# Last FFN: the scale columns made inside VectorE's step operations, in place of three GpSimd products a batch; FFN 0: two GpSimd products in one

## The reference

```python
# FFN 0
def rms_norm(x): return (x - mean(x)) / sqrt(var(x) + 1e-8)
def activation_quant(x):
    s = 127.0 / max(abs(x), axis=-1)
    return clip(round(s * x), -128, 127) / s
xq = activation_quant(rms_norm(x))
out = ternary(silu(ternary(xq, W_g)) * ternary(xq, W_u), W_d)      # matmuls with sign(W)

# last FFN
def act_quant(x):
    scale = 128 / clip(max(abs(x), axis=-1), 1e-5)
    return clip(round(x * scale), -128, 127) / scale
def weight_quant(w):
    scale = 1 / clip(mean(abs(w)), 1e-5)
    return clip(round(w * scale), -1, 1) / scale
gate, up = act_quant(x) @ weight_quant(w_gate).T, act_quant(x) @ weight_quant(w_up).T
h = fwht(silu(gate) * up)              # normalised Walsh-Hadamard transform over 1024
out = act_quant(h) @ weight_quant(w_down).T
x = layernorm(x + out)
```

## Time and profile before

| | |
|---|---|
| median of 3 runs | 720.35 us (719.85 to 720.46) |
| the profiled execution | 719.75 us |
| its span | 717.8 us |
| busy in the span | TensorE 687.1, VectorE 604.6, GpSimd 540.1, ScalarE 410.9 us |
| FFN 0 | about 217 to 340 us |
| last FFN | first `f_e` at 527.5 us, last step of the tail at 713 us; the convolution's last product on TensorE at 582.6 us |

### The profile page before, as it was taken

How to read it: one execution, slowest core, us unless ns; L and a number is a source line. 1 busy time by engine, 2 the same in 40 slices (tenths; PEclk the granted TensorE clock), 3 DMA queues, 4 the chain that set the end, 5 groups by cost and what they waited for, 6 DMA issues and landing times. The chain is left out here.

```text
span 717.8 us, 13771 instructions
## 1 busy us (share of the span) xinstructions
PE 687.1 (96%) x4278; PEld 498.4 (69%) x4302; DVE 604.6 (84%) x1281; ACT 410.9 (57%) x660; POOL 540.1 (75%) x781
## 2 busy tenths in 40 slices
PE   6999999999999999999889999999999999999994
PEld 5888888755444677778668778874544458777883
DVE  2987879679999987755899999988999998878874
ACT  0566667711160654544689978980000358888985
POOL 1878979889877445351067978999998989999963
PEclk9999999999999999999999999999999999999998
DMA  7820000000400041000031211204000000000001
GB/s 272 350 101 3 2 2 2 2 1 2 175 0 1 0 170 56 1 1 2 5 124 52 81 58 44 85 1 136 1 0 1 0 2 1 9 16 16 24 16 45
DMA packets 12727, 33.39 MB, mean 47 GB/s; under 512 B 2672, under 2 KB 8048, under 8 KB 11376
## 3 DMA queue, kind: packets, MB, share of 16 engines
q1 hardware_dynamic: 12656, 32.52, 12.5%
HBM read 30.35 MB, written 2.16 MB: 45 GB/s over the span
## 5 line engine op out<-in xcount | busy, mean ns | idle before, releaser
L1053 PE MATMUL bank<-XT,win_late 128*128 128x256 f32 x320 | 79.3, 385 | 2.2 <-DVE ss_xc L1238 1.8
L619 DVE TENSOR_REDUCE MIX<-m_pr 128x128 f32<-128x1024 f32 x64 | 76.8, 1208 | 0.7 <-issue 0.2
L1238 DVE SCALAR_TENSOR_TENSOR ss_xc<-bank,cw_late,ss_xc 128x254 f32<-128x254 f32 x144 | 67.7, 476 | 3.9 <-ACT ss_xc L1142 0.4
L564 POOL TENSOR_TENSOR m_kv<-CTXT 128x512 f32<-128x512 f32 x64 | 65.1, 1042 | 7.5 <-PE bank L596 6.5
L564 POOL TENSOR_TENSOR m_kv<-XT,CTXT 128x512 f32<-128x512 f32 x64 | 67.1, 1076 | 2.3 <-PE bank L596 2.3
L594 PE MATMUL bank<-m_kv,toep 128*128 128x512 f32 x128 | 65.9, 596 | 0.9 <-DVE ss_ysum L1261 0.8
L1053 PEld LDWEIGHTS bank<-XT,win_late 128*128 128x128 f32 x320 | 57.2, 190 | 11.7 <-DVE ss_xc L1238 3.6
L595 PE MATMUL bank<-m_kv,toep 128*128 128x512 f32 x128 | 65.4, 592 | 0.0
L596 PE MATMUL bank<-m_kv,toep 128*128 128x512 f32 x128 | 65.4, 592 | 0.0
L750 PE MATMUL bank<-wd,f_pmt 128*128 128x256 f32 x256 | 60.4, 379 | 0.0
L1530 PE MATMUL bank<-had_last,f_ht 128*128 128x256 f32 x256 | 58.9, 379 | 0.0
(11 more groups left out here) (247 smaller groups left out, 1869.8 us busy)
## 6 DMA issues: line engine op xcount, KB each, us to landing
MIX<-cum_rows SPq DMA_DIRECT2D x15, 512.0 KB, 3.6
toep<-toep_dram SPq DMA_DIRECT2D x2, 2048.0 KB, 12.4
X<-x_dram SPq DMA_DIRECT2D x1, 2048.0 KB, 13.0
CTXT<-ctxT_dram SPq DMA_DIRECT2D x1, 2048.0 KB, 17.8
out_dram<-f_o SPq DMA_DIRECT2D x16, 128.0 KB, 1.7
XT<-xT_dram SPq DMA_DIRECT2D x1, 1280.0 KB, 8.7
win_late<-win_dram SPq DMA_DIRECT2D x1, 1280.0 KB, 5.2
wgu<-wgu_dram SPq DMA_DIRECT2D x1, 1024.0 KB, 5.3
```

The lines of the kernel that those rows point to most:

```text
L564: m = nc.gpsimd.tensor_tensor(KV[n % 3][:, c, :, :].rearrange("p (b j) i -> p b j i", b=HB), ki, vj, ALU.mult)
L619: nc.vector.tensor_reduce(head(MIX)[:, :, a, bass.ts(h, HB), :], PR[n % 2][:, :, :, :].rearrange("p c (b j) i -> p c b j i", b=HB), op=ALU ...
L1053: m = nc.tensor.matmul(bX[(NU * g + n) % 3][:, 0:GS_], win[:, h, off:off + P], XT[:, h, bass.ts(g, GS_)], start=(h == 0), stop=(h == C - 1))
L1238: m = nc.vector.scalar_tensor_tensor(acc[:, :, sh:S], bank[:, :, 0:S - sh], cw[:, r, n:n + 1], acc[:, :, sh:S], ALU.mult, ALU.add)
```

## The change

In the last FFN, `step_size` becomes one SCALAR_TENSOR_TENSOR on three columns: the peak, spread over the three, max 1e-5, times a constant row of three, `w128` = (1/128, mean of gate/128, mean of up/4096). Its three results are the step and the columns for `silu` and `multiply`. `v_step` does the same with two columns: the step and the column for `add_down`. `gate_scale`, `up_scale` and `down_scale` go, with their semaphores; who waited for those now waits for the step operation. ScalarE makes the constants once, three activations in place of one, and GpSimd fills the two that are 1/128 with two memsets at its entry to the stage. In FFN 0, `f_va` and `f_vb` become one TENSOR_SCALAR with two multiplications.

```diff
@@ mixer, scalar consts @@
-            nc.scalar.activation(T["ws32"][:, :], T["wscale"][:, 1:2], ACT.Identity, scale=1.0 / 32).then_inc(s["made"], 1)
+            for k, m, scale in ((1, 0, 1.0 / 128), (2, 1, 1.0 / 4096), (4, 2, 1.0 / 128)):
+                made = nc.scalar.activation(T["w128"][:, k:k + 1], T["wscale"][:, m:m + 1], ACT.Identity, scale=scale)
+            made.then_inc(s["made"], 1)
...
@@ ffn0, gpsimd rms @@
-            nc.gpsimd.tensor_tensor(VA[k][:, :], MV[k][:, 1:2], RS[k][:, :], ALU.mult).then_inc(s["va"], 1)
-            pool.wait_ge(s["va"], n + 1)
-            nc.gpsimd.tensor_tensor(VB[k][:, :], VA[k][:, :], RS[k][:, :], ALU.mult).then_inc(s["vb"], 1)
+            nc.gpsimd.tensor_scalar(VB[k][:, :], MV[k][:, 1:2], RS[k][:, :], RS[k][:, :], ALU.mult, ALU.mult).then_inc(s["vb"], 1)
...
@@ ffn1, scalar silu @@
-            act.wait_ge(s["gs_made"], n + 1)
+            act.wait_ge(s["inv_made"], n + 1)
...
@@ ffn1, vector step_size @@
-            upto(dve, s["us_made"], n - 3)
-            upto(dve, s["gs_made"], n - 3)
+            upto(dve, s["h1_made"], n - 3)
+            upto(dve, s["silu1_made"], n - 3)
             upto(dve, s["scaled"], n - 3)
-            nc.vector.tensor_scalar(INV[n % 4][:, :], MX[n % 2][:, :], 1e-5, 1.0 / 128, ALU.max, ALU.mult).then_inc(s["inv_made"], 1)
+            if n == 0:
+                dve.wait_ge(mixed["made"], 2)
+                dve.wait_ge(s["consts"], 1)
+            nc.vector.scalar_tensor_tensor(IN3[n % 4][:, :], MX[n % 2][:, :].broadcast_to([P, 3]), 1e-5, w128[:, 0:3], ALU.max, ALU.mult).then_inc(s["inv_made"], 1)
...
@@ ffn1, vector multiply @@
-            dve.wait_ge(s["us_made"], n + 1)
...
@@ ffn1, vector v_step @@
-            upto(dve, s["fs_made"], n - 3)
-            nc.vector.tensor_scalar(HI[n % 4][:, :], HM_[n % 4][:, :], 1e-5, 1.0 / 128, ALU.max, ALU.mult).then_inc(s["hi_made"], 1)
+            upto(dve, s["down_free"], n - 3)
+            upto(dve, s["sh_made"], n - 3)
+            nc.vector.scalar_tensor_tensor(HI2[n % 4][:, :], HM_[n % 4][:, :].broadcast_to([P, 2]), 1e-5, w128[:, 3:5], ALU.max, ALU.mult).then_inc(s["hi_made"], 1)
...
@@ gpsimd_order @@
-    n.mix(28); n.mix(29); n.mix(30); g.edge(6); g.gate_scale(2); n.mix(31); g.rstd(3); g.first(0); g.up_scale(1); g.second(0); g.edge(7)
-    g.up_scale(2); g.gate_scale(3); g.up_scale(3); g.rstd(4); g.first(1); g.second(1); g.rstd(5); g.gate_scale(4); g.up_scale(4); g.edge(8)
+    n.mix(31); g.rstd(3); g.first(0); g.second(0); g.edge(7); g.rstd(4); g.first(1); g.second(1); g.rstd(5); g.edge(8); g.first(2); g.second(2)
```

More of the change, by code:

```diff
@@ L658, in ffn0 @@
     ST3, MV3, VE3, RS3 = two("st3", [P, 6]), two("mv3", [P, 2]), two("ve3", [P, 1]), two("rs3", [P, 1])
-    VA, VB, VC, RS2 = two("va", [P, 1]), two("vb", [P, 1]), two("vc", [P, 1]), two("rs2", [P, 1])
+    VB, VC, RS2 = two("vb", [P, 1]), two("vc", [P, 1]), two("rs2", [P, 1])
     MX, MS, SC, INV = two("mx", [P, 1]), two("ms", [P, 1], n=4), two("sc", [P, 1]), two("inv", [P, 1], n=4)
@@ L815, in aggregate @@
                 return
-            upto(dve, s["va"], n - 1)
+            upto(dve, s["vb"], n - 1)
             upto(dve, s["normed"], n - 1)
@@ L962, in last_tiles @@
 def last_tiles(ch, T):
-    for n, shape in (("bo", [P, P]), ("had", [P, 2, 2 * P]), ("grp", [P, P]), ("bias", [P, 1]), ("ws32", [P, 1])):
+    for n, shape in (("bo", [P, P]), ("had", [P, 2, 2 * P]), ("grp", [P, P]), ("bias", [P, 1]), ("w128", [P, 5])):
         T[n] = ch.sb(n + "_last", shape)
@@ L1398, in two @@
         return [ch.sb(f"f1_{name}{k}", shape, dt) for k in range(n)]
-    bo, had, ws32 = (T[n] for n in ("bo", "had", "ws32"))
+    bo, had = T["bo"], T["had"]
     rnd, unrnd = ch.sb("f1_rnd", [P, 1]), ch.sb("f1_unrnd", [P, 1])
@@ L1410, in ffn1 @@
     MX, SC = two("mx", [P, 1]), two("sc", [P, 1])
-    INV, GS, US, HM_, HI, SH, FS = (two(n, [P, 1], n=4) for n in ("inv", "gs", "us", "hm", "hi", "sh", "fs"))
+    IN3, HI2 = two("in3", [P, 3], n=4), two("hi2", [P, 2], n=4)
+    HM_, SH = (two(n, [P, 1], n=4) for n in ("hm", "sh"))
+    INV, GS, US = ([v[:, k:k + 1] for v in IN3] for k in range(3))
+    HI, FS = ([v[:, k:k + 1] for v in HI2] for k in range(2))
+    w128 = T["w128"]
     b5, b0, b1, b4, b2, b3, bW, bQ = T["banks"]
@@ L1743, in add_down @@
             dve.wait_ge(s["downed"], n + 1)
-            dve.wait_ge(s["fs_made"], n + 1)
             upto(dve, s["o_made"], n - 1)
@@ L1768, in enter @@
             pool.wait_ge(before["x_kept"], B)
+            for k in (0, 3):
+                nc.gpsimd.memset(w128[:, k:k + 1], 1.0 / 128)
             nc.gpsimd.memset(rnd[:, :], ROUND)
@@ L1784, in edge @@
             nc.gpsimd.tensor_tensor(E[n % 2][:, :], X[:, n, :], ctx_row(T, n), ALU.mult).then_inc(s["skip_in"], 1)
[L1786 to L1807, removed]
         def rstd(n):
@@ L1825, in rstd3 @@
             nc.gpsimd.tensor_scalar(NR3[k][:, :], MV3[k][:, 0:1], RS3[k][:, :], -1.0, ALU.mult, ALU.mult).then_inc(s["offset3"], 1)
-        return calls(enter=enter, first=first, second=second, edge=edge, gate_scale=gate_scale, up_scale=up_scale, down_scale=down_scale, rstd=rstd,
+        return calls(enter=enter, first=first, second=second, edge=edge, rstd=rstd,
                      rstd3=rstd3)
@@ L2143, in gpsimd_order @@
     g.enter(); g.edge(0); n.mix(16); g.edge(1); n.mix(17); n.mix(18); n.mix(19); n.mix(20); n.mix(21); n.mix(22); g.edge(2); n.mix(23); g.rstd(0)
-    n.mix(24); g.rstd(1); g.edge(3); n.mix(25); g.up_scale(0); g.edge(4); g.rstd(2); n.mix(26); g.gate_scale(0); n.mix(27); g.edge(5); g.gate_scale(1)
-    n.mix(28); n.mix(29); n.mix(30); g.edge(6); g.gate_scale(2); n.mix(31); g.rstd(3); g.first(0); g.up_scale(1); g.second(0); g.edge(7)
-    g.up_scale(2); g.gate_scale(3); g.up_scale(3); g.rstd(4); g.first(1); g.second(1); g.rstd(5); g.gate_scale(4); g.up_scale(4); g.edge(8)
@@ L2147, in gpsimd_order @@
[L2147 to L2154, removed]
@@ L2155, in gpsimd_order @@
-    g.first(14); g.up_scale(15); g.down_scale(10); g.second(14); g.down_scale(11); g.rstd3(9); g.rstd3(10); g.down_scale(12); g.down_scale(13)
-    g.down_scale(14); g.rstd3(11); g.down_scale(15); g.rstd3(12); g.rstd3(13); g.rstd3(14); g.rstd3(15)
+    n.mix(24); g.rstd(1); g.edge(3); n.mix(25); g.edge(4); g.rstd(2); n.mix(26); n.mix(27); g.edge(5); n.mix(28); n.mix(29); n.mix(30); g.edge(6)
+    n.mix(31); g.rstd(3); g.first(0); g.second(0); g.edge(7); g.rstd(4); g.first(1); g.second(1); g.rstd(5); g.edge(8); g.first(2); g.second(2)
@@ new lines, in gpsimd_order @@
+    g.rstd(6); g.first(3); g.edge(9); g.rstd(7); g.second(3); g.rstd3(0); g.first(4); g.second(4); g.rstd(8); g.first(5); g.edge(10); g.second(5)
+    g.rstd(9); g.first(6); g.rstd3(1); g.second(6); g.edge(11); g.rstd(10); g.edge(12); g.first(7); g.rstd3(2); g.second(7); g.rstd(11); g.edge(13)
+    g.first(8); g.rstd3(3); g.second(8); g.rstd(12); g.rstd3(4); g.first(9); g.second(9); g.edge(14); g.rstd(13); g.first(10); g.second(10)
+    g.rstd3(5); g.rstd(14); g.edge(15); g.first(11); g.second(11); g.rstd3(6); g.rstd(15); g.first(12); g.second(12); g.rstd3(7); g.first(13)
@@ L2159 @@
+    g.second(13); g.rstd3(8); g.first(14); g.second(14); g.rstd3(9); g.rstd3(10); g.rstd3(11); g.rstd3(12); g.rstd3(13); g.rstd3(14); g.rstd3(15)
 AT = ("weights_in later_in pool_consts consts proj_in value_in out_in bv_spread bias_made bp_made "
@@ L2164 @@
       "g0_made g1_made u0_made u1_made silu0_made silu1_made p0_made p1_made p0_turned p1_turned p0_kept p1_kept "
-      "downed down_free stats31 stats3 eps_added3 rstd3 normed3 x_turned x_kept va vb vc rstd2 inv_made").split()
+      "downed down_free stats31 stats3 eps_added3 rstd3 normed3 x_turned x_kept vb vc rstd2 inv_made").split()
 SS = ("rows_made ones_set unit_made tap3_made tap tapped xc_made xs_turned xs_kept xds_made xdt_made cb_made cbm_made args_made floored exped m_made "
@@ L2169 @@
 F1 = ("consts mix_turned skip_made skip_free summed stats1 stats2 eps_added rstd offset normed peaks inv_made scaled shifted "
-      "q_made q_turned q_kept g0_made g1_made u0_made u1_made silu0_made silu1_made gs_made us_made "
+      "q_made q_turned q_kept g0_made g1_made u0_made u1_made silu0_made silu1_made "
       "h0_made h1_made s1_half s1_made s2_half s2_made h0_turned h1_turned h0_kept h1_kept v0_made v1_made v0_kept v1_kept "
-      "v_peaks hi_made sh_made fs_made rounded w_made w_turned w_kept downed down_free "
+      "v_peaks hi_made sh_made rounded w_made w_turned w_kept downed down_free "
       "stats31 stats3 eps_added3 rstd3 offset3 o_made skip_in").split()
```

## The result

The changed kernel takes 725.78 us in the median of 6 runs (724.94 to 727.53) against 720.33 us (6 runs, 718.77 to 720.46): a ratio of 1.0084, interval [1.0069, 1.0099]. It is slower, by 5.45 us where 2.05 was forecast, and lies above the range.

A forecast was written before the change was run, and what follows sets the result against it. TensorE's order was taken as the bound until about 703 us. The terms 1.2 + 1.4 - 0.6 + 0.05 = +2.05 us on 720.35 gave 722.4 us, range 718.9 to 725.0.

The forecast's parts named there:

- TensorE bounds, both feeders close behind: Last FFN: TensorE's order bounds until about 703 us, with GpSimd busy 76.6 and VectorE 65.3 of 80 us.
- FFN 0 at 0: FFN 0: merging two GpSimd products saves about 0.2 us a batch, covered by GpSimd's waiting, so 0.
- The step operation is held until GpSimd's instruction ends, +11.6 us: Last FFN: two-SBUF-tensor step operations on VectorE wait out GpSimd's running instruction, 29 x 0.4 = 11.6 us blocked.
- Term (1): 577.6 to 586.5 us: held `step_size(3)` and `step_size(4)` delay TensorE directly by 1.2 us; bounds 0 and 1.4.
- The wait itself, which I said would be over 1 us: TensorE's wait for VectorE's `m_pr` at 586.66, 0.48 us before the change, was to exceed 1 us.
- Term (2): After 592 us: 9.6 us of holding meets 14.7 us of idle VectorE; 15% passes, 1.4 us; bounds 0 and 3.8.
- Term (3): Last FFN: relief of GpSimd and lost waits close a quarter of TensorE's 2.4 us of gaps, -0.6 us.
- GpSimd's busy time, a sign: Whole kernel: GpSimd's busy time was to fall by some 10 us if the prediction was right.
- Term (4): Tail: `v_step(15)` runs with GpSimd idle, +0.05 us; bounds 0 and 0.1.
- much slower: Last FFN: VectorE holds GpSimd in turn, blocked time passes at 40%, 725.5 us; chance counted within 0.56 for slower.
- Faster: Last FFN: GpSimd's 6.7 us of relief closes nearly all of TensorE's gaps, 718.3 us; chance 0.13.
- Held, but hidden: Last FFN: waits fall into VectorE's idle time, or three columns are not held, about 720.1 us; chance 0.31.

The follow-up runs named there:

- e6_extra_ops: Kernel before with its products and waits, plus 48 unused one-column TENSOR_SCALARs on VectorE behind the step operations; 723.34 us, ratio 1.0056.
- e10_fewer_ops: Kernel before with 32 fewer VectorE instructions, GpSimd's 48 products taking the peak as longer TENSOR_SCALARs with the floor; 727.09 us, ratio 1.0108.
- e1_ffn0_only: Kernel before with only FFN 0's edit, two GpSimd products made one instruction; 719.17 us, ratio 0.9996.
- e3_form_only: Kernel before, products and waits kept, both one-column step operations reading 1/128 from a second SBUF tensor; 725.90 us, ratio 1.0086.
- e2_one_input: Changed kernel with step operations as TENSOR_SCALARs of three and two columns, constants the only tensor, peak a scalar operand; 727.47 us, ratio 1.0112.
- e5_two_forms: Kernel before with `step_size` a three-column TENSOR_SCALAR with immediates, `v_step` one column with the peak as scalar operand; 724.61 us in one run (before 718.94).
- e7_no_products: Changed kernel with the old one-column immediate step operations, and neither the added columns nor GpSimd's products; 720.62 us, ratio 1.002.
- e9_pad: Changed kernel plus 48 one-column VectorE memsets in the first stage, where VectorE waits for the first product; 724.79 us, ratio 1.0077.
- e11_skip_psum: Kernel before with the skip product written back to its PSUM bank, so `skip_add` reads one tensor from PSUM; 718.40 us, ratio 0.9989.
- e4_pointer_scalars: Changed kernel with each step operation split into one-column TENSOR_SCALARs, constants of the other columns as scalar operands; 722.80 us, ratio 1.0035.

## Why the prediction was wrong, step by step

- *TensorE bounds, both feeders close behind:* right. The windows, e6_extra_ops and e10_fewer_ops show both as near the bound.
- *FFN 0 at 0:* right (e1_ffn0_only).
- *The step operation is held until GpSimd's instruction ends, +11.6 us:* right in mechanism and nearly in size. It was +10.3, means of 459 and 487 ns, ends 0.02 us after GpSimd's; 11.8 in e3_form_only. The condition, two tensors from SBUF, was too narrow: one tensor of three columns is held as well (e2_one_input, e5_two_forms).
- *Term (1), 1.2 us before 586.66:* nearly in size, in part by luck. TensorE's transposes moved from 586.66 to 587.22. At the first transposes of the stage after was 0.33 us ahead (536.79 against 537.12), so it had lost 0.9 us. `step_size(3)` took 0.83 us and `step_size(4)` 0.67, as worked out, but `skip_add`, 1.49 us at 581.98 in before, took 0.67 there and gave 0.8 us back. In turn `step_size(0)` to `(2)`, put at 0, took 0.39, 0.63 and 0.37 us, and VectorE had lost 0.5 us by 577.79. The wait itself, which I said would be over 1 us, stayed at 0.43: the delay had come in earlier.
- *Term (2), "I let 15% through", 1.4 us:* this is the step that failed. After 592 us the step operations were held for 8.2 us (what each took over 0.15 us), near the 9.6 forecast, but from 586.66 to `v_step(15)` the changed kernel fell from 0.6 to 5.4 us behind. That is 4.9 us with the relief of term (3) already taken off, so some 60% or more went through in place of 15%. Of e3_form_only's held time 51% went through. I set 9.6 us of holding against 14.7 us of idle VectorE and took the idle time for slack. It took in less than half. Where VectorE of after is idle it waits for its partners (second fence below), and the holding falls into the busy runs between, ahead of a multiply or a rounding that TensorE needs (661.91, 594.17, 684.82). It also pushes other instructions of VectorE behind a butterfly: 2.6 us are lost that way between 594.17 and 599.27, of which 0.5 are won back by 602. Even the bound of 40% was too low.
- *Term (3), relief of GpSimd, -0.6:* by itself nothing (e7_no_products, +0.3 to 0.6 of span at like clock); beside a loaded VectorE -0.4 to -0.9, so the size was right there. It is inside the 4.9 us. GpSimd's busy time, a sign that I put at some 10 us less, fell by 7.1.
- *Term (4), the tail:* right, 0.17 us.
- *Not in the sum:* about 1 us outside the span, which is gone with 48 instructions more (e9_pad); its cause stays open.
- *The rivals:* "much slower", 725.5 us, has the price, though not the whole of the mechanism: GpSimd, with less to do, did not fall behind by its own work, it waited more for VectorE (in before 2.5 and 1.7 us for these two, beside 8.3 us for `f_hi` that went with the products). Waits of after from 560 to 724 us (us, times, longest), GpSimd's here and VectorE's below:

```profile
POOL f_veo L461 <- DVE f_mvo L1766: 14.2, 6, 8.8
...
POOL f_ve L461 <- DVE f_mv L1669: 7.2, 7, 2.0
```

```profile
DVE f_hm L1724 <- ACT f_v L1605: 6.2, 8, 1.3
...
DVE f_ydown L1752 <- ACT f_o L1627: 3.8, 4, 2.7
DVE f_ydown L1752 <- PE bank L1555: 2.9, 4, 1.3
```

"Faster" fell with e7_no_products: without the products the span is no shorter, so the 2.4 us of TensorE's gaps do not come from them. "Held, but hidden" fell with TensorE's 4.85 us of idle time.

## What to carry to other kernels

Where two feeders run near full beside the bound, read idle time as the partner's turn and not as slack: here half to three quarters of what was added to VectorE or GpSimd reached the end. What was taken away returned nothing on GpSimd (e7_no_products); on VectorE, 1.6 us less returned about 1 us (e11_skip_psum). Before an instruction moves to VectorE beside a busy GpSimd, ask what it reads: two SBUF tensors, or one of more than one column in a TENSOR_SCALAR, made it wait here for the end of GpSimd's instruction however small it was; one tensor of one column, or a PSUM operand in place of the second tensor, did not. Look at the execution's time beside the span as well, since a change of the instruction list moved that by a microsecond.

## What the runs showed of the hardware

- An instruction of one to three columns is held up to 1.2 to 1.3 us (e3_form_only, e5_two_forms), eight times its own 0.15.
- GpSimd's power instruction did not hold the step operations that met it. In after, the first row of VectorE runs inside the row of GpSimd below it and takes its usual time:

```profile
595.34 0.16 DVE L1688 SCALAR_TENSOR_TENSOR f_in<-f_mx,w_last 128x3 f32<-128x3 f32 x1
...
595.18 0.55 POOL L463 TENSOR_TENSOR f_rs<-f_ve,mhalf 128x1 f32<-128x1 f32 x1
```

- The same instruction took longer beside two long ones of VectorE. In before it takes 1.19 us in place of 0.55 while `skip_add` and `f_w` run (595.00 and 595.53 above), and ends 0.04 us after `f_w`:

```profile
595.07 1.19 POOL L463 TENSOR_TENSOR f_rs<-f_ve,mhalf 128x1 f32<-128x1 f32 x1
```

- A scalar operand from a tile costs VectorE 204 ns in place of 147 on one column (e4_pointer_scalars), and a GpSimd product of one column 320 to 490 ns as TENSOR_SCALAR with two operations in place of 190 to 220 as TENSOR_TENSOR (e10_fewer_ops); how much of the latter is VectorE holding GpSimd, as in the earlier trace rows, was not separated.
